# Two-layer graph kernel, one core: half of a strip's fourth part is turned as a bf16 high half on TensorE with its low half by DMA

## The reference, cut to what matters

```
h = max(layernorm(x), 0)
q, k, v = h @ Wq.T + bq, h @ Wk.T + bk, h @ Wv.T + bv
scores = where(adj > 0, q @ k.T / sqrt(128), -9e15)      # 4096 x 4096
x = x + elu(softmax(scores) @ v)
```

## Time and profile before

| | us |
|---|---|
| median of 3 runs (range) | 771.36 (771.25 to 771.85) |
| the profiled execution, its own time | 769.68 |
| its span, first to last instruction | 767.9 |
| first strips of the attention to its last TensorE work | about 52 to 478 |
| second layer's chain on TensorE to the end | 528 to 764 |

### The profile page before, as it was taken

One profiled execution on the slowest core, in us unless ns is written; L12 is line 12 of the kernel. 1 busy time (PEld: TensorE's weight loads), 2 busy tenths in 40 slices (PEclk: granted clock), 3 DMA queues, 4 the chain that ended last, 5 costly groups with the idle time before them and its releaser, 6 DMA issues. The chain is left out here.

```text
span 767.9 us, 18394 instructions
## 1 busy us (share of the span) xinstructions
PE 731.9 (95%) x6301; PEld 616.8 (80%) x6301; DVE 564.3 (73%) x1199; ACT 549.4 (72%) x1063; POOL 432.9 (56%) x349
## 2 busy tenths in 40 slices
PE   8979999999999999999999997785999999999996
PEld 7658888888888888888888886554888888888885
DVE  5968787878878787877878784698477576577572
ACT  3846868787786878777786867685877977987910
POOL 5688799999999999999999963351000000000000
PEclk9989999999999999999999999697999999999999
DMA  6189998998979898887989742820253534433100
GB/s 234 60 286 252 243 269 240 280 252 253 258 251 262 235 279 238 276 257 245 258 252 269 220 97 56 168 53 0 63 91 65 94 76 80 92 74 80 38 10 13
DMA packets 189324, 130.88 MB, mean 170 GB/s; under 512 B 170336, under 2 KB 176992, under 8 KB 181088
## 3 DMA queue, kind: packets, MB, share of 16 engines
q1 hardware_dynamic: 188544, 130.05, 62.1%
q10 hardware_dynamic: 576, 0.26, 0.1%
q0 software_dynamic: 160, 0.00, 0.0%
HBM read 69.47 MB, written 18.87 MB: 115 GB/s over the span
## 5 line engine op out<-in xcount | busy, mean ns | idle before, releaser
L1381 PE MATMUL ps_x<-v,big 128*128 128x258 bf16 x2048 | 232.2, 275 | 2.3 <-issue 2.3
L1381 PEld LDWEIGHTS ps_x<-v,big 128*128 128x128 fp8e4 x2048 | 199.0, 98 | 32.6 <-issue 2.4
L726 DVE CUSTOM_DVE_ANT_0 scores<-ps_s,mask_neg 128x1024 f32<-128x1024 f32 x128 | 155.8, 1217 | 17.3 <-POOL mask_neg L309 17.0
L647 ACT ACTIVATE scores<-scores,neg_max 128x1024 f32<-128x1024 f32 x128 | 146.1, 1143 | 17.8 <-DVE neg_max L732 17.8
L745 DVE TENSOR_TENSOR low<-scores 128x1024 bf16<-128x1024 f32 x96 | 136.8, 1425 | 28.6 <-ACT scores L647 28.6
L309 POOL TENSOR_SCALAR mask_neg<-mask_bytes 128x2048 bf16<-128x2048 uint8 x64 | 153.3, 2396 | 5.4 <-POOL mask_bytes L304 0.4
L304 POOL TENSOR_SCALAR mask_bytes<-adj_sb 128x2048 uint8<-128x2048 int32 x64 | 148.2, 2332 | 3.4 <-POOLq L80 1.7
L661 ACT ACTIVATE hiT<-ps_t 128x512 bf16<-128x512 bf16 (+1 forms) x128 | 103.0, 805 | 53.4 <-PE ps_t L837 50.7
L856 PE MATMUL ps_acc<-v_parts,hiT 128*128 128x256 bf16 x768 | 140.4, 273 | 0.7 <-DMA lowT<-low 0.4
L922 ACT ACTIVATE big<-s_block,s_col 128x512 fp8e4<-128x512 f32 x224 | 139.4, 717 | 0.0
L857 PE MATMUL ps_acc<-v_parts,lowT 128*128 128x128 bf16 x768 | 133.6, 219 | 0.0
(11 more groups left out here) (144 smaller groups left out, 1010.3 us busy)
## 6 DMA issues: line engine op xcount, KB each, us to landing
adj_sb<-in_adj SPq DMA_DIRECT2D x64, 1024.0 KB, 5.3
mask_bytes_dram<-mask_bytes SPq DMA_DIRECT2D x32, 512.0 KB, 2.9
x_sb<-in_x SPq DMA_DIRECT2D x8, 256.0 KB, 7.8
out<-res SPq DMA_DIRECT2D x32, 64.0 KB, 1.6
lowT<-low SPq DMA_TRANSPOSE x96, 4.7
big<-mask_bytes_dram SPq DMA_TRANSPOSE x32, 4.6
raw_w<-in_L_gnn_Wq ACTq DMA_DIRECT2D x1, 64.0 KB, 3.2
raw_w<-in_L_gnn_Wk ACTq DMA_DIRECT2D x1, 64.0 KB, 3.8
```

Source lines behind the costliest of these rows:

```text
L647: nc.scalar.activation(sc, sc, ACT.Exp, bias=neg_max[:, bn:bn + 1], accum_out=row_sum[:, bn, k:k + 1]).then_inc(exp_done, 1)
L726: nc.vector.tensor_tensor_reduce(out=scores[bn % 2][:, part(k)], in0=ps_s[k % 2][:], in1=mask[bn % 2][:, part(k)], scale=1.0, scalar=LOWES ...
L1381: last = nc.tensor.matmul(ps_x[b % 2][k][:], by_key_tile(m, t)[:, b], v1[k][:, t, :].bitcast(BF16), start=(t == 0), stop=(t == T - 1))
```

## The change

The second half of part 3 (columns 3584 to 4095) is no longer turned as f32. Its high half is turned on TensorE by four bf16 transposes, its low half is made by VectorE from the f32 scores in SBUF (a fourth `low_part`, 128x512) and turned by a fourth DMA transpose into `lowT3`. The first half of part 3 stays as it was: f32 transposes, `pT_high`, `turned_low`. The epilogue (`acc_copy`, `add_halves`, `elu_exp`, `add_elu`) is the same.

The core of the diff:

```diff
+            UNITS = ((3, slice(0, 512)), (3, slice(512, PART)), (0, slice(0, PART)), (1, slice(0, PART)),
+                     (2, slice(0, 512)), (2, slice(512, PART)))
...
+                pT_high, pT_low = (sb(c2, f"pT_{n}", [D, 512], BF16) for n in ("high", "low"))
+                hiT = [sb(c2, f"hiT{k}", [D, PART], BF16) for k in range(3)] + [sb(c2, "hiT3", [D, 512], BF16)]
+                low = [sb(c2, f"low{k}", [D, PART], BF16) for k in range(3)] + [sb(c2, "low3", [D, 512], BF16)]
+                lowT = [sb(c2, f"lowT{k}", [D, 8, D], BF16) for k in range(3)] + [sb(c2, "lowT3", [D, 4, D], BF16)]
...
                     def turn_low(c, b, k):
-                        sp.wait_ge(low_done, 3 * s + k + 1)
+                        sp.wait_ge(low_done, 4 * s + 1 + (1, 2, 3, 0)[k])
...
                         if has(c, b, 1):
+                            turn_low(*at(c, b, 1), 3)
                             turn_low(*at(c, b, 1), 0)
...
+                        if u == 0:
+                            nc.scalar.activation(pT_high[:], ps_t[0][:], ACT.Copy).then_inc(hiT_ready, 1)
+                        else:
+                            out = hiT[3][:] if u == 1 else hiT[k][:, half_of]
+                            nc.scalar.activation(out, ps_t[u % 3][:].bitcast(BF16)[:, half_of], ACT.Copy).then_inc(hiT_ready, 1)
...
-                        turned_low(s, 0)
+                        turned_low(s)
                         low_part(s, b, 1)
                         if ahead:
                             add_mask(s + 1, bn, 2)
-                        turned_low(s, 1)
                         low_part(s, b, 2)
...
                         if ahead:
+                            low_part(s + 1, bn, 3)
                             low_part(s + 1, bn, 0)
...
                     def times_v(s, i):
                         j = PV_ORDER[i]
+                        pe.wait_ge(hiT_ready, TURNS * s + (1, 2, 3, 3, 4, 4, 5, 6)[i])
+                        if i == 0:
+                            pe.wait_ge(pT_low_ready, s + 1)
+                        elif i == 1 or i % 2 == 0:
+                            pe.wait_ge(lowT_in[j // 2], 16 * s + 16)
```

More of the change, by code:

```diff
@@ L743, in low_part @@
                         wait(dve, lowT_in[k], 16 * s)
-                        p = scores[b % 2][:, part(k)]
+                        p = scores[b % 2][:, part(k) if k < 3 else slice(N - 512, N)]
                         nc.vector.tensor_tensor(low[k][:], p, high_half(p), ALU.subtract).then_inc(low_done, 1)
@@ L766, in _ @@
                     add_mask(1, 1, 0)
+                    low_part(0, 0, 3)
+                    add_mask(1, 1, 1)
                     low_part(0, 0, 0)
-                    add_mask(1, 1, 1)
                     def period(c, b):
@@ L813, in make_scores, with turn @@
                         last.then_inc(s_ready, 1)
-                    def turn(s, b, i):
-                        pe.wait_ge(exp_done, 4 * s + 1)
-                        wait(pe, hiT_ready, 4 * (s - 1) + 2 + i)
-                        for t in range(4):
-                            col = 512 * (6 + i) + D * t
-                            last = nc.tensor.transpose(ps_t[i % 3][:, D * t:D * t + D], scores[b % 2][:, col:col + D], ident[:])
-                        last.then_inc(t_done, 1)
-                    def turn_high(s, b, u):
-                        k, tiles = ((0, range(8)), (1, range(8)), (2, range(4)), (2, range(4, 8)))[u]
+                    def turn(s, b, u):
+                        k, half_of = UNITS[u]
                         pe.wait_ge(exp_done, 4 * s + EXP_ORDER.index(k) + 1)
+                        wait(pe, hiT_ready, TURNS * s + u - 2)
                         if u == 0:
-                            wait(pe, hiT_ready, 4 * s)
-                        elif u < 3:
-                            pe.wait_ge(pT_low_ready, 2 * s + u)
-                        else:
-                            pe.wait_ge(hiT_ready, 4 * s + 1)
-                        out = ps_t[(2 + u) % 3][:].bitcast(BF16)
+                            for t in range(4):
+                                col = 512 * 6 + D * t
+                                last = nc.tensor.transpose(ps_t[0][:, D * t:D * t + D], scores[b % 2][:, col:col + D], ident[:])
+                            last.then_inc(t_done, 1)
+                            return
+                        if u == 3:
+                            pe.wait_ge(pT_low_ready, s + 1)
+                        out = ps_t[u % 3][:].bitcast(BF16)
                         high = high_half(scores[b % 2][:, part(k)])
-                        for t in tiles:
-                            last = nc.tensor.transpose(out[:, D * t:D * t + D], high[:, D * t:D * t + D], ident_half[:])
+                        for col in range(half_of.start, half_of.stop, D):
+                            last = nc.tensor.transpose(out[:, col:col + D], high[:, col:col + D], ident_half[:])
                         last.then_inc(t_done, 1)
@@ L884, in period @@
                             make_scores(s + 2, b % 2, 0)
-                        turn_high(s, b, 2)
+                        turn(s, b, 4)
                         times_v(s, 2)
@@ L889, in period @@
                             make_scores(s + 2, b % 2, 1)
[L890 removed]
+                        turn(s, b, 5)
                         times_v(s, 4)
```

61 lines of the change are left out of this document (23 added, 38 removed).

## The result

The kernel after takes **803.96 us** (median of 6 runs, 800.29 to 805.45) against 771.46 for the kernel before in the same comparison (6 runs, 770.93 to 773.95): a ratio of 1.0407, 95% interval 1.0379 to 1.0434. The forecast was 788, slower; it is slower, by 32 us where 16 had been worked out. Put on the 771.36 us from which the forecast started, the ratio gives 771.36 x 1.0407 = 802.8, at the very top of its range, which reached up to 803. The profiled execution took 801.17 us, span 799.4 (before 769.68 and 767.9).

What follows compares the result with a forecast made beforehand. TensorE was taken to set the 13.32 us beat, GpSimd about 0.1 behind. Late `lowT3`, GpSimd's 0.45 and VectorE's 0.1 gave 13.96: 27 x 0.64 - 1.0 = +16.3, so 788 us; range from below 779 up to 803.

Steps and rivals of the forecast that it cites:

- TensorE, 0.20 a strip: TensorE's turns: four bf16 transposes in place of four f32 ones save 0.20 us a strip, 6.4 us over 32.
- rival "faster": GpSimd loses nothing and `lowT3` lands in time, so TensorE's 0.20 us a strip counts: 765 us; chance 0.07.
- GpSimd, 0.45 a strip: `low3` excludes GpSimd where it makes its bytes: 0.45 us a strip, bounds 0 to 0.97.
- longer ones as a sign of being right: GpSimd's second half of the bytes, or the instruction ahead of it, was to take longer with `low3` beside it.
- rival "only the exclusion": `lowT3` lands in time, so GpSimd's beat of 13.65 us sets the time: 779 us; chance 0.22.
- VectorE's own waits, taken as 0.1: One more `low_part` that may wait for GpSimd, 0 to 0.48 us; mostly covered, so 0.1 added to the beat.
- rival "worse": VectorE's two adjacent subtractions each wait for GpSimd, up to 1.9 us, and TensorE's waits grow: beat 14.4, 800 us; chance 0.09.
- The cover that it counted on: VectorE's idle time, 0.88 us before `low0` and 0.94 before the next `pT_low`, was to cover `low3`'s some 0.6 us.
- `lowT3` late by 0.1 to 1.1: `lowT3` lands behind an `adj` load, so TensorE's second block of products waits about 0.6 us (0.1 to 1.1).
- the ring that sets the beat: Loop over two strips: GpSimd's bytes, load, `lowT3`, TensorE, ScalarE's last copy, elu, GpSimd; 13.86 us a strip.
- The sum: Attention beat 13.96 us, 0.64 over 13.32, 27 times; five other strips gain 0.2 each: +16.3 us, 786.0 profiled, 788 median.
- Second layer: The second layer, from 528 us, should keep its length.

Runs made afterwards that it cites:

- both costs taken away: Kernel after with `low3` cut from 512 to 8 columns and without the DMA transpose `lowT3` and its waits: 770.94 us, 0.9983 to the kernel before.
- joint version: Kernel after with TensorE's second product block and next scores exchanged, and `low3` and `low0` made by one 1536-column subtraction: 775.65 us, 1.0061 to the kernel before.

## Why the prediction was right in its sign and too small

- **TensorE, 0.20 a strip: right** (0.45 - 0.24), and right that it is worth little: with both costs taken away the time is 770.94, and GpSimd, which the forecast put right behind TensorE, is at 95.02. The rival "faster" (765) had no room.
- **GpSimd, 0.45 a strip: the size was right, the place in the sum wrong.** 0.46 in the joint version, 4.19 - 3.75 = 0.44 in the kernel after. But in the kernel after GpSimd idles 3.09 and 0.68 us in two strips: it pays from time that it has. And its bytes are shorter there than in the kernel before (3.75 and 4.19 against 4.72), while the forecast had named longer ones as a sign of being right: where GpSimd had waited for VectorE, VectorE now waits for GpSimd. Only in the joint version, where nothing else is late, is it the ring that bounds; that is the rival "only the exclusion" (779, a beat of 13.65), measured 775.65 with beats of 13.5.
- **VectorE's own waits, taken as 0.1: here the forecast failed.** The text had the mechanism, but as its rival "worse" ("two adjacent subtractions each wait for a GpSimd instruction", a beat of 14.4 and 800 us, at 0.09), and in every second strip that is what came. In the sum it priced `low3` as one more subtraction that waits as the others do, mostly covered, and not the pair: `low3` waits, lets go, GpSimd begins its next half, `low0` waits again. The second wait makes the pair 5.14 - 3.32 = 1.82 us longer in every second strip, and the beats of two strips differ by 15.45 - 13.29 = 2.16: 1.1 a strip instead of 0.1. 27 x 1.0 = 27 us is more than the whole gap to the forecast, since what the forecast took for the late `lowT3` falls away. The cover that it counted on was real, but the new waits of some 2.6 us a strip use it up. On this the Trainium skill (page "SBUF — State Buffer", section "SBUF: two separate sides") says that whichever of the two starts first keeps the port pair for its whole instruction. The trace agrees: `low0` of the pair of 5.14 us ends 255.42 + 5.14 - 259.48 = 1.08 us behind GpSimd's second half, less than its own length of 1.2, so it didn't run before. The forecast had used the rule for GpSimd's loss, and for VectorE's only at 0.1.
- **`lowT3` late by 0.1 to 1.1: right as a wait** (0.57 and 1.46), wrong as the ring that sets the beat: from 131.86 us on the beat is the same without it (344.72 against 344.86 us over 24 beats). The 8.5 us that go without it, or with TensorE wanting it later, come for the most part from two long waits near the start (6.62 and 3.24 us), which the sum had not looked at. Where VectorE doesn't bound, it costs 14.1.
- **The sum** took 0.64 a strip, about half of it from the late `lowT3` (0.62 over two strips is 0.31), 0.22 from GpSimd and 0.1 from VectorE; the trace has 1.05, from VectorE's waits. So 786 + 27 x 0.41 = 797 for the profiled execution, and the 4 us from there to its 801.17 are the start. Slower would have followed from GpSimd's term alone (779). That 788 lies nearer to the result is luck: its largest term is nothing in the beat, and another, taken at 0.1, stands in its place.
- **Second layer:** its length is kept; the span behind the last `add_elu` differs by under 2 us.

Not shown by an experiment: why the strips settle into exactly this alternation. The time lines fit the account that a strip with two waits makes ScalarE, and so GpSimd's next round, late, so that `low3` then meets the second half.

## What to carry to other kernels

An operation that excludes another engine cost here its own length plus the rest of whatever that engine had just begun, and two of them back to back paid twice where the other engine began its next instruction between them. Price such an edit by laying the two engines' time lines over one another at the very place, and for the pair, not as an average over all instances; joining the two into one, or moving one to where the other engine has only short instructions, gave back 17 to 20 us of 24 here. And look at the first pass of a pipeline apart from its beat, since TensorE waited for the late transfer 6.6 and 3.2 us there, which cost time, and 0.4 to 1.9 us later on, which cost none.

## What the runs showed of the hardware that was not expected

- A VectorE subtraction of 8 columns with both operands in SBUF took 1784 ns at the median beside GpSimd's byte instructions, 146 at best.
- GpSimd's half mask of 1024 columns takes 1.047 us where 2048 take 1.90, so cutting one in two costs 2 x 1.047 - 1.90 = 0.19. And GpSimd then lost more to the exclusion than in the kernel after, not less: 5.54 and 5.02 us of bytes in two strips instead of 3.75 and 4.19.
- The same 512 columns subtracted once more a strip cost 34 us at one place of VectorE's order (805.35) and 1.4 or nothing at another (772.38, interval 0.9993 to 1.0036).
